# A graph and mixture-of-experts layer on one Trainium2 core: row distances moved from VectorE and ScalarE sweeps to TensorE turnings and products with ones

## The chip, the cores and the metric

The kernel runs on one core of a Trainium2 chip. The metric is device time in microseconds (us), the median of several executions. TensorE's matmuls are called PE in the rows, the weight loads before them PEld, VectorE DVE, ScalarE ACT, GpSimd POOL, and the queue of SyncE SP.

## The reference

The input is x, 12500 rows of 256 float32, and 200000 edges (src, dst), sorted by dst. The layer has two halves. What the change touches is in the first:

```python
mems  = layernorm(x)
mems2 = mems.at[y].set(r)                        # one row is overwritten by r
d2    = sum((mems2 - r)**2, axis=-1)             # distance of every row to r
nbr   = top_k(-d2, 7)                            # 7 nearest rows become edges into row y
deg   = segment_sum(keep, dst) + 2.0             # edges into y are dropped, the 7 added
dinv  = rsqrt(deg)
out   = segment_sum(dinv[src] * dinv[dst] * (mems2 @ W)[src], dst) + 2 * dinv**2 * (mems2 @ W)
x     = x + out
```

The second half is layernorm again, a gate that picks one of 8 experts per row, at most 1954 rows an expert, two matmuls 256 to 1024 to 256, and the result times its gate added to x.

## The kernel before, in words

The program is written by hand with semaphores: each engine has its own list of instructions, and each wait names a semaphore and a count. Nothing reorders it. The 12500 rows lie as 98 windows of 128 rows (`NW`) in one tile `nodes`, 128 partitions x 2 halves of 128 features (`KD`) x 98 windows x 128. Windows go in 7 chunks of 14 (`NZC`, `ZC`), or in 14 batches of 7 (`U`). `arena` is a tile that many buffers share in turn, and `columns` holds per-row numbers. The stages up to the first gather, which the change is about:

- SyncE loads edges and x (L495 to L518). TensorE turns the edges and their limits (L1701, L1708); VectorE copies them out (L984, L1001).
- VectorE works out bases and keys of the groups of edges from the limits (L1003 to L1063). In the middle it signals `bases`; TensorE spreads them over the partitions by three products with ones (L1711 to L1714, `cmp_ps`), and VectorE goes on with the keys.
- Then the row statistics (L1065 to L1097): `bn_stats` of 98 windows, ScalarE's root (L761), and scale and shift per row. Normalising in place: ScalarE windows 0 to 39 (`ACT_WIN`, L754), VectorE 40 to 97 (L1100). VectorE patches row y with r (L1105).
- Beside it GpSimd fetches 98 rows of sorted dst (L654), seven a batch, and ScalarE counts in them (`count_first`, L750), 9 batches (`EARLY`) ahead of the root and 5 between its normalising. When all 98 are counted (`less_ok`), VectorE and two products on TensorE (L1718, L1719) make the degrees, ScalarE their root, VectorE `dinv` (L1172, `deg_ok`).
- Distances and scaling, woven together: VectorE subtracts r from 7 windows (`differ`, L1114), ScalarE squares (L775), VectorE sums (`sum_squares`, L1122); and each chunk of `nodes` is multiplied by `dinv`, chunks 0, 2, 4, 6 on VectorE (L1181), 1, 3, 5 on ScalarE (L779). The scaled rows are called z. SyncE stores each chunk to `z_table` in DRAM as soon as it is scaled (L527).
- When a chunk is stored, TensorE turns its windows (L1743), and VectorE (L1195) and ScalarE (L790) write them back to `nodes` as the start of the sums.
- VectorE takes the 7 smallest distances in a few steps (L1203 to L1232) that run among the first gathers.

After that GpSimd gathers rows of `z_table` by src (L669), 4 tiles of 128 edges a step, 304 steps, with 4 buffers; TensorE adds each step up by a product with a selection matrix (L1776), VectorE adds it into `nodes` (L1248). GpSimd starts when all chunks are stored and all distances are done (L659 to L661). Convolution, layernorm, gate and routing run among the later steps, and the experts follow (L2017, L2029).

```python
            for c in range(NZC):
                pool.wait_ge(chunk_moved[c], STORED[c])
            pool.wait_ge(S["dist_ok"], 2 * NZC)
```

Of the kernel before, what the change touches and what calls it, by code (L numbers as in the profile page):

```python
# [10 lines left out]
P = 128  # L11


def build(nc, x, src, dst, gnn_r, gnn_w, yidx, gate_w, gate_b, w1, b1, w2, b2, out):
# [77 lines left out]
    ACT_WIN = 40  # L92
    EARLY = 9
    NEAR_PE, NEAR_DVE = (0, 4, 7), (2, 5, 8)
    DR = 4
    LAG = DR - 1

# [88 lines left out]
    with ctx:  # L186
# [10 lines left out]

        up_bank = [bank[2], bank[3], bank[6], bank[7]]
# [121 lines left out]
        at[0] = here - EB * P  # L320
        cross_row = carve([TILES])[0:1, :]
        at[0] = here + 16 * P // 2
# [10 lines left out]
        at[0] = 0  # L333
        diff = carve([DR, U, KD, P])

# [81 lines left out]
        dist = sb("dist", [P, NW])  # L417
        first_i = sb("first_i", [P, NW], I32)
# [39 lines left out]
        for name in ("""edges_cleared edges_in r_in y_in consts edges_float edge_psum edges_out lims limps lim_rows bases  # L458
                     cmp_ps hist_built hist_used hist_ps mean_sum square_ok ssum dst_rows_out last_built first_ok
                     first_in0 first_in1 half_ok starts_ok starts_ps hist_start less_ok bn1_ok shift_ok  # L460
                     piece_out piece_turned mem_ok mem_patched diff_ok dist_ok deg_ok z_ok z_act tick near_ok near_ps chosen_ok zT_ps
# [29 lines left out]
        def _(sp):  # L491
# [29 lines left out]
            for c in range(NZC):  # L521
                if c % 2:
                    sp.wait_ge(S["z_act"], (c + 1) // 2 * ZC)
                else:
                    sp.wait_ge(S["z_ok"], c // 2 + 1)
# [84 lines left out]
        def _(pool):  # L610
# [50 lines left out]
            pool.wait_ge(S["dist_ok"], 2 * NZC)  # L661
# [77 lines left out]
        def _(act):  # L739
            def node_row(w):  # L740
                return nodes[:, :, w, :]
# [11 lines left out]
            def normalise(w):  # L753
                nc.scalar.activation(node_row(w), node_row(w), ACT.Identity, bias=shift[:, w:w + 1],  # L754
                                     scale=rstd[:, w:w + 1]).then_inc(S["mean_sum"], 1)

            act.wait_ge(S["half_ok"], 1)
            for b in range(EARLY):
                count_first(b)
            act.wait_ge(S["ssum"], 1)  # L760
            nc.scalar.activation(dist[:, :], var2[:, :], ACT.Sqrt).then_inc(S["root_ok"], 1)  # L761
            act.wait_ge(S["shift_ok"], 1)
            part = -(-ACT_WIN // (2 * NZC - EARLY))
# [4 lines left out]
            act.wait_ge(S["mean_sum"], ACT_WIN)  # L768
            act.sem_inc(S["mem_ok"], 1)
            act.wait_ge(S["deg_ok"], 1)  # L770
            nc.scalar.activation(deg_root[:, :], deg[:, :], ACT.Sqrt).then_inc(S["root_ok"], 1)

            for b in range(2 * NZC):
                act.wait_ge(S["diff_ok"], KD * (b + 1))
                nc.scalar.activation(diff[:, b % DR, :, :, :], diff[:, b % DR, :, :, :], ACT.Square).then_inc(S["square_ok"], 1)  # L775
                if b % 4 == 3:
                    act.wait_ge(S["deg_ok"], 2)
                    for w in range(b // 2 * ZC, (b // 2 + 1) * ZC):
                        nc.scalar.activation(node_row(w), node_row(w), ACT.Identity, bias=zeros[:, 0:1],  # L779
                                             scale=dinv[:, w:w + 1]).then_inc(S["z_act"], 1)  # L780

            act.wait_ge(S["dst_kept"], 16)
            act.wait_ge(S["less_ok"], NW)
            nc.scalar.activation(counts_f, zeros[:, 0:1].to_broadcast([P, P * NW // 2]), ACT.Copy).then_inc(S["counts_clear"], 1)
# [9 lines left out]
            act.wait_ge(S["dist_ok"], 2 * NZC)  # L794
# [140 lines left out]
        def _(dve):  # L935
# [62 lines left out]
            for n in range(len(EDGE_TURNS)):  # L998
                i, b0, nb = EDGE_TURNS[n]
                dve.wait_ge(S["limps"], n + 1)  # L1000
                then(nc.vector.tensor_copy(lim_row[0:1, i, b0 * P:(b0 + nb) * P], bank[2 + n % 2][0:1, 0:nb * P]))  # L1001
                dve.sem_inc(S["lim_rows"], 1)
            lim_grp = lim_row[0:1, :, 0:TILES].rearrange("p i (g t) -> p i g t", t=GT)  # L1003
# [61 lines left out]
            dve.wait_ge(S["r_in"], 16)  # L1065
            then(nc.vector.memset(rel_b[:, TILES:EB * P], -1.0))
            then(nc.vector.tensor_single_scalar(wy_i[:, :], y_i[:, :], 7, ALU.arith_shift_right))
            then(nc.vector.tensor_scalar(is_y[:, :], node_id[:, :], y_f[:, 0:1], None, ALU.is_equal))
            then(nc.vector.tensor_scalar(not_y[:, :], is_y[:, :], -1.0, 1.0, ALU.mult, ALU.add))
            then(nc.vector.tensor_reduce(mine_y[:, :], is_y[:, :], AX.X, ALU.add))  # L1070
            then(nc.vector.tensor_scalar(r_y[:, :], r_rows[:, :], mine_y[:, 0:1], None, ALU.mult))
            then(nc.vector.tensor_scalar(invalid[:, :], node_id[:, :], float(N), -3.0e38, ALU.is_ge, ALU.mult))
            then(nc.vector.tensor_scalar(tok_id[:, :], node_id[:, :], 1.0, None, ALU.add))
            then(nc.vector.memset(taken_i[:, :], 0))


            for c in range(NZC):
                dve.wait_ge(chunk_moved[c], LOADED[c])
                for w in range(c * ZC, (c + 1) * ZC):
                    nc.vector.bn_stats(bn1[:, w, :], nodes[:, :, w, :]).then_inc(S["bn1_ok"], 1)  # L1080
            dve.wait_ge(S["bn1_ok"], NW)
            then(nc.vector.tensor_tensor(gap2[:, :], bn1[:, :, 1], bn1[:, :, 4], ALU.subtract))
            then(nc.vector.tensor_tensor(gap2[:, :], gap2[:, :], gap2[:, :], ALU.mult))
            then(nc.vector.tensor_tensor(var2[:, :], bn1[:, :, 2], bn1[:, :, 5], ALU.add))
            then(nc.vector.tensor_scalar(var2[:, :], var2[:, :], 1.0 / D, EPS, ALU.mult, ALU.add))
            then(nc.vector.scalar_tensor_tensor(var2[:, :], gap2[:, :], 0.25, var2[:, :], ALU.mult, ALU.add))
            dve.sem_inc(S["ssum"], 1)
            then(nc.vector.tensor_tensor(neg_mean[:, :], bn1[:, :, 1], bn1[:, :, 4], ALU.add))
            then(nc.vector.tensor_scalar(neg_mean[:, :], neg_mean[:, :], -0.5, None, ALU.mult))
            dve.wait_ge(S["root_ok"], 1)  # L1090
            then(nc.vector.reciprocal(rstd[:, :], dist[:, :]))
            then(nc.vector.tensor_tensor(gap2[:, :], rstd[:, :], rstd[:, :], ALU.mult))
            then(nc.vector.tensor_tensor(gap2[:, :], gap2[:, :], var2[:, :], ALU.mult))
            then(nc.vector.tensor_scalar(gap2[:, :], gap2[:, :], -0.5, 1.5, ALU.mult, ALU.add))
            then(nc.vector.tensor_tensor(gap2[:, :], gap2[:, :], not_y[:, :], ALU.mult))
            then(nc.vector.tensor_tensor(rstd[:, :], rstd[:, :], gap2[:, :], ALU.mult))
            nc.vector.tensor_tensor(shift[:, :], rstd[:, :], neg_mean[:, :], ALU.mult).then_inc(S["shift_ok"], 1)  # L1097
            dve.wait_ge(S["shift_ok"], 1)
            for w in range(ACT_WIN, NW):
                nc.vector.tensor_scalar(nodes[:, :, w, :], nodes[:, :, w, :], rstd[:, w:w + 1], shift[:, w:w + 1],  # L1100
                                        ALU.mult, ALU.add).then_inc(S["mem_ok"], 1)
            wy = dve.value_load(wy_i[0:1, 0:1], min_val=0, max_val=NW - 1)
            dve.wait_ge(S["mem_ok"], NW - ACT_WIN + 1)
# [4 lines left out]

            def differ(b):

                if b >= DR:
                    dve.wait_ge(S["dist_ok"], b - DR + 1)
                for k in range(KD):
                    nc.vector.tensor_tensor(diff[:, b % DR, :, k, :], nodes[:, k, b * U:(b + 1) * U, :],  # L1114
                                            r_rows[:, k * P:(k + 1) * P].unsqueeze(1).to_broadcast([P, U, P]),
                                            ALU.subtract).then_inc(S["diff_ok"], 1)
                if b >= LAG:
                    sum_squares(b - LAG)

            def sum_squares(b):  # L1120
                dve.wait_ge(S["square_ok"], b + 1)
                nc.vector.tensor_reduce(dist[:, b * U:(b + 1) * U], diff[:, b % DR, :, :, :], AX.XY, ALU.add).then_inc(S["dist_ok"], 1)  # L1122
# [20 lines left out]
            with dve.If(n_unsorted > 0):  # L1143
                nc.vector.tensor_copy(dst_i[:, :], dst_f[:, :]).then_inc(S["hist_start"], 1)
# [29 lines left out]
            differ(0)  # L1174
            differ(1)
            dve.wait_ge(S["deg_ok"], 2)
            for c in range(NZC):
                for k in range(KD if c % 2 == 0 else 0):
                    dve.wait_ge(S["diff_ok"], 2 * KD * (c + 1))
# [3 lines left out]
                if c % 2 == 0:  # L1183
                    ins.then_inc(S["z_ok"], 1)
# [900 lines left out]
```

## Time and profile before

| | |
|---|---|
| median of 3 runs | 2591.44 us (2588.29 to 2591.5) |
| the profiled execution | 2592.29 us |
| its span, first to last instruction | 2590.8 us |
| granted TensorE clock, mean | 0.888 |
| TensorE busy / weight loads | 1964.7 us (76%) / 1697.6 us (66%) |
| VectorE busy | 1318.2 us (51%) |
| ScalarE busy | 1011.5 us (39%) |
| GpSimd busy | 1548.2 us (60%) |
| first gather of z (L669) | at 246.96 us |

A page of a profile gives busy time as a mean over the whole span, and this program has stages with different limits. So the views used below are cut by time: the instructions of a stretch in order (the timeline, in which neighbours of one line are merged and "idle before" names what ended the wait), the groups of a line in a stretch, and the busy time of each engine in a stretch with the granted clock of TensorE. A clock of 1.00 is 2.4 GHz, 0.50 is 1.2 GHz.

### The profile page before, as it was taken

To read this page: it belongs to the slowest core of one execution; us is meant where nothing else is said; L and a number is where in the kernel's file an instruction comes from. 1 tells how busy PE (TensorE), PEld (TensorE's weight loads), DVE (VectorE), ACT (ScalarE), POOL (GpSimd) and SP (SyncE) were. 2 spreads that over 40 slices of the span, in tenths; PEclk is the share of its full clock that TensorE was granted. 3 is DMA by queue.
4 is the path that set the end of the run, shared out by engine and by line. 5 is a ranking of instruction groups with operands and counts; after the bars stand their busy time and mean duration, and the time that the engine had idled before them with its cause. 6 is when DMAs were issued, how large, how long until landed. Compare 5 with 4: busy or idle time off the path is not lost. (4 is left out here: it accounts for less than half of the span.)

```text
span 2590.8 us, 36610 instructions
## 1 busy us (share of the span) xinstructions
PE 1964.7 (76%) x11096; PEld 1697.6 (66%) x11096; DVE 1318.2 (51%) x3683; ACT 1011.5 (39%) x1769; POOL 1548.2 (60%) x1612
## 2 busy tenths in 40 slices
PE   2002777866786796786878888998599999999995
PEld 1002655855675585675767788887488788788875
DVE  7969875255325425335242257776444444454443
ACT  1377555345425525435343133333232323322332
POOL 6631777777777777777777777776223422422234
PEclk8555888988898898898989999999699999999998
DMA  9216433743473474573756777777512212212121
GB/s 264 66 57 181 120 103 115 259 136 104 152 253 106 128 254 128 165 240 104 238 166 206 229 213 208 210 208 173 143 33 71 83 36 71 76 36 71 42 68 28
DMA packets 235522, 359.05 MB, mean 139 GB/s; under 512 B 46585, under 2 KB 172697, under 8 KB 235221
## 3 DMA queue, kind: packets, MB, share of 16 engines
q0 software_dynamic: 74176, 194.10, 26.3%
q1 hardware_dynamic: 159860, 160.86, 20.2%
q10 hardware_dynamic: 1312, 2.10, 0.3%
q8 instruction: 71, 1.16, 0.2%
q14 instruction: 103, 0.84, 0.1%
HBM read 305.38 MB, written 56.40 MB: 140 GB/s over the span
## 5 line engine op out<-in xcount | busy, mean ns | idle before, releaser
L669 POOL DMA_INDIRECT arena<-z_table,arena x1216 | 1185.4, 975 | 462.0 <-issue 361.6
L1776 PE MATMUL bank<-arena 128*128 128x128 f32 x4864 | 711.0, 307 | 267.2 <-DMA arena<-z_table,arena 143.4
L1776 PEld LDWEIGHTS bank<-arena 128*128 128x128 f32 x4864 | 662.1, 218 | 364.3 <-issue 293.1
L1248 DVE TENSOR_TENSOR nodes<-nodes,bank 128x256 f32 x304 | 128.1, 421 | 755.8 <-PE bank L1776 740.8
L729 POOL DMA_INDIRECT out<-arena x128 | 130.7, 1021 | 419.1 <-DVE arena L1660 396.6
L2017 PE MATMUL bank<-arena 128*128 128x256 f32 (+1 forms) x1472 | 330.2, 384 | 14.2 <-DVE arena L1608 8.9
L927 ACT ACTIVATE nodes<-bank,arena 128x256 f32<-128x256 f32 (+1 forms) x368 | 152.7, 466 | 457.5 <-PE bank L2017 457.5
L2029 PE MATMUL bank<-arena,nodes 128*128 128x256 f32 (+1 forms) x1472 | 326.0, 379 | 0.0
L2017 PEld LDWEIGHTS bank<-arena 128*128 128x128 f32 x1472 | 282.7, 196 | 55.1 <-DVE arena L1608 10.9
L817 ACT ACTIVATE arena<-iota_h,arena 128x490 f16<-128x490 f16 x280 | 194.6, 695 | 304.3 <-PE bank L1788 304.3
L2029 PEld LDWEIGHTS bank<-arena,nodes 128*128 128x128 f32 (+1 forms) x1472 | 272.6, 187 | 40.1 <-issue 1.0
L1798 PE MATMUL bank<-arena,columns 128*128 128x256 f32 x1176 | 271.9, 381 | 2.7 <-ACT columns L807 2.7
L807 ACT ACTIVATE columns<-arena 128x768 f32<-128x768 uint16 (+3 forms) x102 | 153.1, 1506 | 262.2 <-PE bank L1798 258.8
L1798 PEld LDWEIGHTS bank<-arena,columns 128*128 128x128 f32 x1176 | 217.6, 192 | 29.2 <-issue 3.3
L1238 DVE TENSOR_TENSOR arena<-iota_b,arena 128x512 f32<-128x512 bf16 x304 | 208.5, 687 | 0.1
L819 ACT ACTIVATE arena<-arena,ones 128x490 bf16<-128x490 f16 x280 | 196.9, 703 | 9.1
L1268 DVE TENSOR_TENSOR arena<-arena,bank 128x490 f32 x280 | 184.8, 660 | 3.0 <-issue 1.3
L718 POOL DMA_INDIRECT arena<-x_rows,list_i x128 | 125.2, 978 | 98.9 <-DVEq L1597 49.8
L1608 DVE COPY arena<-bank 128x512 f32<-128x512 f32 (+1 forms) x46 | 31.2, 679 | 218.8 <-PE bank L1999 215.8
L1788 PE MATMUL bank<-arena 128*128 128x490 bf16 x352 | 119.4, 435 | 16.7 <-DVE arena L1268 14.9
L654 POOL DMA_INDIRECT arena<-dst_rows,first_i x98 | 100.7, 1027 | 52.1 <-issue 29.3
L1640 DVE TENSOR_TENSOR arena<-bank,arena 128x256 f32<-128x256 f32 x92 | 39.0, 424 | 146.9 <-PE bank L2029 142.7
(315 smaller groups left out, 1850.8 us busy)
## 6 DMA issues: line engine op xcount, KB each, us to landing
arena<-z_table SPq DMA_DIRECT2D x96, 768.0 KB, 4.6
arena<-z_table,arena POOLq DMA_INDIRECT x1216
arena<-in_L_ffn_w SPq DMA_DIRECT2D x14, 1024.0 KB, 7.0
z_table<-nodes SPq DMA_DIRECT2D x14, 896.0 KB, 6.7
x_rows<-nodes SPq DMA_DIRECT2D x98, 128.0 KB
arena<-in_x SPq DMA_DIRECT2D x48, 256.0 KB, 3.1
out<-nodes SPq DMA_DIRECT2D x96, 128.0 KB
nodes<-in_x SPq DMA_DIRECT2D x12, 896.0 KB, 11.5
```

The source lines that it names most:

```text
L669: nc.gpsimd.indirect_dma_start(gath[:, slot, t, :], None, z_table, bass.IndirectOffsetOnAxis(ap=src_idx[:, tile_at:tile_at + 1], axis=0)). ...
L729: nc.gpsimd.indirect_dma_start(out, bass.IndirectOffsetOnAxis(ap=out_idx[0:m, 2 * n + t:2 * n + t + 1], axis=0), o_tile[0:m, slot, :], Non ...
L807: nc.scalar.activation(count_f[:, j, 0:m, 0:nodes_in], counts[:, 0:nodes_in, c * HB:c * HB + m].rearrange("p n h -> p h n"), ACT.Copy).the ...
L817: nc.scalar.activation(far, iota_h[:, :], ACT.Abs, bias=neg_key[:, n:n + 1]).then_inc(S["key_ok"], 1)
L819: nc.scalar.activation(oh_key[:, n % 2, t, :], far, ACT.Relu, bias=ones[:, 0:1], scale=-1.0).then_inc(S["key_ok"], 1)
L927: nc.scalar.activation(hid[:, f, 0:n], up_bank[f // 2][:, f % 2 * CR:f % 2 * CR + n], ACT.Relu, bias=b1_pair[:, j * FT + f:j * FT + f + 1] ...
L1238: nc.vector.tensor_tensor(sel[:, step % SR, :, :], iota_b[:, :].unsqueeze(1).to_broadcast([P, GT, P]), rel_b[:, t0:t0 + GT].unsqueeze(2).t ...
L1268: nc.vector.tensor_tensor(where, where, strip_bank[n % 2][:, 0:PW], ALU.add).then_inc(S["strip_added"], 1)
L1776: last = nc.tensor.matmul(agg_bank[i][:, k * P:(k + 1) * P], gath[:, i, t, k * P:(k + 1) * P], sel[:, i, t, :], start=(t == 0), stop=(t == ...
L1798: last = nc.tensor.matmul(piece_bank[:, 0:D], count_f[:, j, i, :], z_ring[:, j, i, :], start=False, stop=False)
L2017: last = nc.tensor.matmul(up_bank[b][:, i * CR:i * CR + n], w1_sb[:, j, k, f * P:(f + 1) * P], xs_feat[:, s % 2, k, 0:n], start=(k == 0), ...
L2029: last = nc.tensor.matmul(bank[4 + t][0:m, 0:D], hid[:, f, t * P:t * P + m], w2_sb[:, j, f, :], start=(f == 0), stop=(f == FT - 1))
```

## The change

The distances are computed otherwise. VectorE no longer subtracts or sums. For each block of 4 windows (`NBK` = 25 blocks, the last of 2) TensorE turns the normalised windows, so that features lie on partitions (`turn_nodes`, two PSUM banks a block, two pairs in turn); ScalarE squares them out of PSUM with minus r as the bias per feature (`far_squares`, into 3 buffers `squares` in the arena); TensorE multiplies each squared 128 x 128 piece by a column of ones, which adds the features up into one column of `dist_bank` per window (`sum_squares`). Minus r per feature comes from turning r once. TensorE's order is turn block b, then sum block b - 1.

So that the rows are normalised early, the statistics are moved ahead of the keys, behind the limits' copies, and VectorE normalises all 98 windows. The bases' spread over partitions moves into TensorE's stream, behind turning block 20. ScalarE counts 6 batches before the root and 8 after it, with up to 4 blocks of squares behind each. Row y is patched only when all windows are turned. Chunks 2 and 5 of z are scaled by ScalarE, the other five by VectorE, one after the other. GpSimd no longer waits for the distances.

```diff
-    ACT_WIN = 40
-    EARLY = 9
+    EARLY = 6
+    NBK = -(-NW // 4)
+    SQ = 3
+    SPREAD_AT = 20
+    Z_ACT = (2, 5)
+    Z_DVE = [c for c in range(NZC) if c not in Z_ACT]
...
+        dist_bank = bank[7]
+        far_bank = [(bank[2], bank[3]), (bank[0], bank[6])]
...
 # gpsimd
-            pool.wait_ge(S["dist_ok"], 2 * NZC)
...
 # scalar
-            def normalise(w):
-                nc.scalar.activation(node_row(w), node_row(w), ACT.Identity, bias=shift[:, w:w + 1],
-                                     scale=rstd[:, w:w + 1]).then_inc(S["mean_sum"], 1)
+            def far_squares(b):
+                wide = P * min(4, NW - 4 * b)
+                act.wait_ge(S["nT_ps"], b + 1)
+                if b >= SQ:
+                    act.wait_ge(S["dist_ps"], b - SQ + 1)
+                for k in range(KD):
+                    nc.scalar.activation(squares[b % SQ][:, k, 0:wide], far_bank[b % 2][k][:, 0:wide], ACT.Square,
+                                         bias=neg_r[:, k:k + 1]).then_inc(S["square_ok"], 1)
...
             for b in range(EARLY, 2 * NZC):
-                for w in range((b - EARLY) * part, min((b - EARLY + 1) * part, ACT_WIN)):
-                    normalise(w)
                 count_first(b)
+                for n in range(4 * (b - EARLY), min(4 * (b - EARLY + 1), NBK)):
+                    far_squares(n)
...
-            for b in range(2 * NZC):
-                act.wait_ge(S["diff_ok"], KD * (b + 1))
-                nc.scalar.activation(diff[:, b % DR, :, :, :], diff[:, b % DR, :, :, :], ACT.Square).then_inc(S["square_ok"], 1)
-                if b % 4 == 3:
...
+            act.wait_ge(S["deg_ok"], 2)
+            for c in Z_ACT:
...
 # vector: the block from wait r_in to the statistics is moved from behind the keys to behind the limits, and ends with
-            for w in range(ACT_WIN, NW):
+            for w in range(NW):
                 nc.vector.tensor_scalar(nodes[:, :, w, :], nodes[:, :, w, :], rstd[:, w:w + 1], shift[:, w:w + 1],
                                         ALU.mult, ALU.add).then_inc(S["mem_ok"], 1)
...
-            dve.wait_ge(S["mem_ok"], NW - ACT_WIN + 1)
+            dve.wait_ge(S["mem_ok"], NW)
+            dve.wait_ge(S["nT_ps"], NBK)
...
-            differ(0)
-            differ(1)
             dve.wait_ge(S["deg_ok"], 2)
-            for c in range(NZC):
-                for k in range(KD if c % 2 == 0 else 0):
-                    dve.wait_ge(S["diff_ok"], 2 * KD * (c + 1))
+            for c in Z_DVE:
+                for k in range(KD):
                     rows = nodes[:, k, c * ZC:(c + 1) * ZC, :]
                     ins = nc.vector.tensor_tensor(rows, rows, dinv[:, c * ZC:(c + 1) * ZC].unsqueeze(2).to_broadcast([P, ZC, P]),
                                                   ALU.mult)
...
 # tensor
+            def turn_nodes(b):
+                pe.wait_ge(S["mem_ok"], min(4 * (b + 1), NW))
+                if b >= 2:
+                    pe.wait_ge(S["square_ok"], KD * (b - 1))
+                for k in range(KD):
+                    for i in range(min(4, NW - 4 * b)):
+                        last = nc.tensor.transpose(far_bank[b % 2][k][:, i * P:(i + 1) * P], nodes[:, k, 4 * b + i, :], ident[:, :])
+                last.then_inc(S["nT_ps"], 1)
+
+            def sum_squares(b):
+                pe.wait_ge(S["square_ok"], KD * (b + 1))
+                for i in range(min(4, NW - 4 * b)):
+                    w = 4 * b + i
+                    for k in range(KD):
+                        last = nc.tensor.matmul(dist_bank[:, w:w + 1], squares[b % SQ][:, k, i * P:(i + 1) * P], ones[:, 0:1],
+                                                start=(k == 0), stop=(k == KD - 1))
+                last.then_inc(S["dist_ps"], 1)
...
+            for b in range(NBK):
+                turn_nodes(b)
+                if b == SPREAD_AT:
+                    spread_bases()
+                if b:
+                    sum_squares(b - 1)
+            sum_squares(NBK - 1)
```

On TensorE, from the spread of the bases to the turning of z, the order before is (`row_start` are the counts, `nodes` at the end is z):

```order
L1712 MATMUL bank<-grp_cmp,ones 128x392 [waits bases]
L1713 MATMUL bank<-arena,ones 128x280
L1714 MATMUL bank<-ones,disorder 1x1
L1718 MATMUL bank<-row_start,down_one 128x98 [waits starts_ok]
L1719 MATMUL bank<-row_start,corner 128x98
```

With the change the same engine has this around the spread and at the end of the distances (`arena` with `ones` are the squares):

```order
L1716 MATMUL bank<-ident,nodes 128x128 [waits square_ok,mem_ok]
L1716 MATMUL bank<-ident,nodes 128x128 x7
L1700 MATMUL bank<-grp_cmp,ones 128x392 [waits bases]
L1701 MATMUL bank<-arena,ones 128x280
L1702 MATMUL bank<-ones,disorder 1x1
L1724 MATMUL bank<-ones,arena 128x1 [waits square_ok]
L1724 MATMUL bank<-ones,arena 128x1 x7
...
L1716 MATMUL bank<-ident,nodes 128x128 [waits square_ok,mem_ok]
L1716 MATMUL bank<-ident,nodes 128x128 x3
L1724 MATMUL bank<-ones,arena 128x1 [waits square_ok]
L1724 MATMUL bank<-ones,arena 128x1 x7
L1724 MATMUL bank<-ones,arena 128x1 [waits square_ok]
L1724 MATMUL bank<-ones,arena 128x1 x3
L1739 MATMUL bank<-row_start,down_one 128x98 [waits starts_ok]
```

Before, the two products of the degrees came right behind the spread; now 196 turnings and 196 products with ones stand ahead of them in TensorE's queue, and the spread stands among these.

On VectorE, at the patch of row y and behind `dinv`, the order before is:

```order
L1105 ISA [waits mem_ok]
L1105 TENSOR_TENSOR nodes<-nodes,r_y 128x128
...
L1172 TENSOR_TENSOR dinv<-dinv,columns 128x98 [waits dve_ch]
L1114 TENSOR_TENSOR arena<-nodes,r_rows 128x7x128 x4
L1181 TENSOR_TENSOR nodes<-nodes,dinv 128x1792 [waits diff_ok,deg_ok]
L1181 TENSOR_TENSOR nodes<-nodes,dinv 128x1792 [waits diff_ok]
L1114 TENSOR_TENSOR arena<-nodes,r_rows 128x7x128 x4
L1122 TENSOR_REDUCE dist<-arena 128x7 [waits square_ok]
```

and with the change:

```order
L1115 ISA [waits nT_ps,mem_ok]
L1115 TENSOR_TENSOR nodes<-nodes,r_y 128x128
...
L1168 TENSOR_TENSOR dinv<-dinv,columns 128x98 [waits dve_ch]
L1174 TENSOR_TENSOR nodes<-nodes,dinv 128x1792 [waits deg_ok]
L1174 TENSOR_TENSOR nodes<-nodes,dinv 128x1792 x9
L1181 TENSOR_SCALAR nodes<-bank 128x2x128 [waits zT_ps,chunk_moved0] x7
```

The patch now waits for the turnings as well, and behind `dinv` VectorE has the scaling of five chunks alone, with the writing back of the turned windows right behind it.

## Rows read from the trace of the kernel before

**Rows 1.** The groups of one line, L669: instructions, shortest/median/longest ns, first and last start.

```profile
L669 POOL DMA_INDIRECT arena<-z_table,arena x1216: 942/946/2245, 247.0 to 1806.7; - x174
```

**Rows 2.** GpSimd's timeline, 240:274: start, duration, line, [idle <- its end].

```profile
272.01 0.94 POOL L669 DMA_INDIRECT arena<-z_table,arena  x1 [5.34 <-PE bank L1776]
```

**Rows 3.** Timeline of all engines, 160 to 248 us.

```profile
164.66 0.18 ACT L750 ACTIVATION_READ_ACCUMULATOR arena<-arena,columns 128x1 f32 x1
...
165.69 0.74 PE L1718 MATMUL bank<-row_start,down_one 128*128 128x98 f32 x2 [88.40 <-DVEq L1128]
...
170.86 0.26 DVE L1172 TENSOR_TENSOR dinv<-dinv,columns 128x98 f32<-128x98 f32 x1
...
175.23 3.96 DVE L1181 TENSOR_TENSOR nodes<-nodes,dinv 128x1792 f32<-128x1792 f32 x2
...
179.22 60.87 SPq L527 DMA_DIRECT2D z_table<-nodes  x14
...
233.11 3.96 DVE L1181 TENSOR_TENSOR nodes<-nodes,dinv 128x1792 f32<-128x1792 f32 x2
...
246.96 0.94 POOL L669 DMA_INDIRECT arena<-z_table,arena  x1 [86.78 <-DMA z_table<-nodes]
```

**Rows 4.** Groups by line, 20:270: xcount | busy, mean ns | idle before.

```profile
L1114 DVE TENSOR_TENSOR arena<-nodes,r_rows 128x896 f32<-128x896 f32 x28 | 29.1, 1087 | 0.3
L1122 DVE TENSOR_REDUCE dist<-arena 128x7 f32<-128x1792 f32 x14 | 28.0, 2014 | 0.0
```

**Rows 5.** Timeline of VectorE, 10 to 270 us.

```profile
50.79 1.10 DVE L1001 COPY arena<-bank 1x512 f32<-1x512 f32 x2 [0.20 <-PE bank L1708]
...
73.90 0.56 DVE L1043 SCALAR_TENSOR_TENSOR grp_cmp<-grp_bad,grp_base 1x392 f32<-1x392 f32 x1
77.33 0.30 DVE L1046 TENSOR_TENSOR arena<-arena,bank 128x144 f32<-128x144 f32 x1 [2.87 <-PE bank L1714]
...
86.00 0.14 DVE L1066 MEMSET arena<- 128x96 bf16 x1
...
88.51 32.11 DVE L1080 BATCH_NORM_STATS2 arena<-nodes 128x6 f32<-128x256 f32 x98
...
125.95 19.69 DVE L1100 TENSOR_SCALAR nodes<-nodes,columns 128x256 f32<-128x256 f32 x58
```

**Rows 6.** Stretches: busy us of PE, PEld, DVE, ACT, POOL; clock, DMA.

```profile
195.00:200.00 5.00, 0.00 (x0) 0.00 (x0) 5.00 (x5) 0.85 (x1) 0.00 (x0) 0.50 1.00 286
```

**Rows 7.** Timeline of weight loads, 1834 to 1843 us.

```profile
1834.75 0.87 PEld L1872 LDWEIGHTS bank<-ident,arena 128*128 128x128 f32 x4
1835.60 1.83 PEld L1881 LDWEIGHTS bank<-arena 128*128 128x128 f32 x8
...
1840.33 1.83 PEld L1881 LDWEIGHTS bank<-arena 128*128 128x128 f32 x8
1842.03 0.97 PEld L1900 LDWEIGHTS bank<-arena 128*128 128x128 f32 x4
```

**Rows 8.** Timeline of weight loads, 1603 to 1608 us.

```profile
1605.25 0.97 PEld L1881 LDWEIGHTS bank<-arena 128*128 128x128 f32 x8
1606.14 1.87 PEld L1776 LDWEIGHTS bank<-arena 128*128 128x128 f32 x16
```

**Rows 9.** Stretches, the turning of z (L1743) alone: busy PE, busy PEld, clock, DMA.

```profile
244.00:247.00 3.00, 3.00 (x16) 3.00 (x15) 0.50 0.55 159
...
251.00:255.00 4.00, 4.00 (x40) 4.00 (x38) 1.00 0.41 109
```

**Rows 10.** Stretches, all engines, columns as in rows 6.

```profile
340.00:390.00 50.00, 36.10 (x199) 27.00 (x200) 31.15 (x93) 24.54 (x37) 38.12 (x40) 0.84 0.36 103
1600.00:1610.00 10.00, 8.84 (x70) 8.20 (x68) 9.19 (x25) 1.64 (x4) 8.17 (x7) 1.00 0.76 207
1831.00:1843.00 12.00, 8.93 (x40) 8.50 (x40) 7.51 (x36) 4.56 (x7) 0.00 (x0) 0.51 0.12 10
```

**Rows 11.** One line, L851, an eviction of 128x512 from PSUM by ScalarE.

```profile
L851 ACT ACTIVATE arena<-bank x49: 571/598/601, 1495.9 to 1836.1; 128x512 f32<-128x512 f32 x49
```

More of the change, by code:

```diff
@@ L319, in build @@
         stage_f2 = carve([EB, P])
-        at[0] = here - EB * P
+        at[0] = 0
         cross_row = carve([TILES])[0:1, :]
+        squares = []
+        for begins in (here - EB * P, here, here + 16 * P // 2 + U * P):
+            at[0] = begins
+            squares.append(carve([KD, 4 * P]))
+        assert at[0] <= here + (2 * 16 * (P + NW)) // 2
         at[0] = here + 16 * P // 2
@@ new lines, in _ @@
+            then(nc.vector.tensor_scalar(r_y[:, :], r_rows[:, :], mine_y[:, 0:1], None, ALU.mult))
+            then(nc.vector.tensor_scalar(invalid[:, :], node_id[:, :], float(N), -3.0e38, ALU.is_ge, ALU.mult))
+            then(nc.vector.tensor_scalar(tok_id[:, :], node_id[:, :], 1.0, None, ALU.add))
+            then(nc.vector.memset(taken_i[:, :], 0))
+            for c in range(NZC):
+                dve.wait_ge(chunk_moved[c], LOADED[c])
+                for w in range(c * ZC, (c + 1) * ZC):
+                    nc.vector.bn_stats(bn1[:, w, :], nodes[:, :, w, :]).then_inc(S["bn1_ok"], 1)
@@ new lines, in _ @@
+            dve.wait_ge(S["bn1_ok"], NW)
+            then(nc.vector.tensor_tensor(gap2[:, :], bn1[:, :, 1], bn1[:, :, 4], ALU.subtract))
+            then(nc.vector.tensor_tensor(gap2[:, :], gap2[:, :], gap2[:, :], ALU.mult))
+            then(nc.vector.tensor_tensor(var2[:, :], bn1[:, :, 2], bn1[:, :, 5], ALU.add))
+            then(nc.vector.tensor_scalar(var2[:, :], var2[:, :], 1.0 / D, EPS, ALU.mult, ALU.add))
+            then(nc.vector.scalar_tensor_tensor(var2[:, :], gap2[:, :], 0.25, var2[:, :], ALU.mult, ALU.add))
@@ new lines, in _ @@
+            dve.sem_inc(S["ssum"], 1)
+            then(nc.vector.tensor_tensor(neg_mean[:, :], bn1[:, :, 1], bn1[:, :, 4], ALU.add))
+            then(nc.vector.tensor_scalar(neg_mean[:, :], neg_mean[:, :], -0.5, None, ALU.mult))
+            dve.wait_ge(S["root_ok"], 1)
+            then(nc.vector.reciprocal(rstd[:, :], dist[:, :]))
+            then(nc.vector.tensor_tensor(gap2[:, :], rstd[:, :], rstd[:, :], ALU.mult))
+            then(nc.vector.tensor_tensor(gap2[:, :], gap2[:, :], var2[:, :], ALU.mult))
@@ new lines, in _ @@
+            then(nc.vector.tensor_scalar(gap2[:, :], gap2[:, :], -0.5, 1.5, ALU.mult, ALU.add))
+            then(nc.vector.tensor_tensor(gap2[:, :], gap2[:, :], not_y[:, :], ALU.mult))
+            then(nc.vector.tensor_tensor(rstd[:, :], rstd[:, :], gap2[:, :], ALU.mult))
+            nc.vector.tensor_tensor(shift[:, :], rstd[:, :], neg_mean[:, :], ALU.mult).then_inc(S["shift_ok"], 1)
+            dve.wait_ge(S["shift_ok"], 1)
+            for w in range(NW):
+                nc.vector.tensor_scalar(nodes[:, :, w, :], nodes[:, :, w, :], rstd[:, w:w + 1], shift[:, w:w + 1],
+                                        ALU.mult, ALU.add).then_inc(S["mem_ok"], 1)
@@ L1081, in _ @@
[L1081 to L1086, printed above, removed]
@@ L1182, in _ @@
                                                   ALU.mult)
-                if c % 2 == 0:
-                    ins.then_inc(S["z_ok"], 1)
-                if c + 1 < NZC:
-                    differ(2 * (c + 1))
-                    differ(2 * (c + 1) + 1)
-            for b in range(2 * NZC - LAG, 2 * NZC):
-                sum_squares(b)
+                ins.then_inc(S["z_ok"], 1)
             for w in range(0, NW, 2):
@@ L1200, in _ @@
             ycol = dve.value_load(y_i[0:1, 0:1], min_val=0, max_val=N - 1)
-            dve.wait_ge(S["dist_ok"], 2 * NZC)
-            then(nc.vector.scalar_tensor_tensor(near[:, :], dist[:, :], -1.0, not_y[:, :], ALU.mult, ALU.mult))
+            dve.wait_ge(S["dist_ps"], NBK)
+            then(nc.vector.scalar_tensor_tensor(near[:, :], dist_bank[:, 0:NW], -1.0, not_y[:, :], ALU.mult, ALU.mult))
             then(nc.vector.tensor_tensor(near[:, :], near[:, :], invalid[:, :], ALU.add))
@@ L1710, in _, with spread_bases @@
                 last.then_inc(S["limps"], 1)
-            pe.wait_ge(S["bases"], 1)
-            nc.tensor.matmul(bank[4][:, 0:GROUPS], ones[0:1, :], grp_cmp[0:1, :], start=True, stop=True)
-            nc.tensor.matmul(bank[5][:, 0:UN], ones[0:1, :], unit_cmp, start=True, stop=True)
-            nc.tensor.matmul(bank[4][0:1, GROUPS:GROUPS + 1], disorder[:, :], ones[:, 0:1], start=True, stop=True).then_inc(S["cmp_ps"], 1)
+            def spread_bases():
+                pe.wait_ge(S["bases"], 1)
+                nc.tensor.matmul(bank[4][:, 0:GROUPS], ones[0:1, :], grp_cmp[0:1, :], start=True, stop=True)
+                nc.tensor.matmul(bank[5][:, 0:UN], ones[0:1, :], unit_cmp, start=True, stop=True)
+                nc.tensor.matmul(bank[4][0:1, GROUPS:GROUPS + 1], disorder[:, :], ones[:, 0:1],
+                                 start=True, stop=True).then_inc(S["cmp_ps"], 1)
@@ new lines, in _ @@
+            pe.wait_ge(S["r_in"], 16)
+            for k in range(KD):
+                last = nc.tensor.transpose(bank[5][:, k * P:(k + 1) * P], r_rows[:, k * P:(k + 1) * P], ident[:, :])
+            last.then_inc(S["r_ps"], 1)
+            def turn_nodes(b):
[6 more added lines that the diff above has]
+                last.then_inc(S["nT_ps"], 1)
```

88 lines of the change are left out of this document (27 added, 61 removed).

## The prediction, made before the changed kernel ran

> **What bounds the kernel now.** I read the gathers first, because every later stage consumes them. GpSimd issues 1216 of them, from 247.0 to 1806.7 us [rows 1], one each 1.25 us with next to no other wait; what follows the last one lasts as long as before, whenever it starts. So the time is the moment of the first gather, plus a chain that this change does not touch, plus the waits inside the chain. There is one such wait worth naming: after 16 gathers GpSimd stands for 5.3 us until TensorE has added up the first group [rows 2], since TensorE could not begin before VectorE and ScalarE had refilled `nodes`. The first gather waits for the last store of the scaled rows z, 86.8 us long [rows 3].
>
> Next, what sets that store. VectorE runs without a gap from the limits (L1001) over the keys to the row statistics and the normalised rows [rows 5]. Then it stands until ScalarE's last count of edges (L750) ends at 164.8 us; the small chain from there to `dinv` ends at 171.1 us [rows 3]. From 171 to 243 us VectorE alternates scaling and distances: 28 subtractions and 14 sums, 57 us [rows 4]. So the stores, which start at 179.2 us, are issued over 61 us [rows 3], though they move 286 GB/s where z is there in time [rows 6]. TensorE has nearly nothing to do in this stage.
>
> **What leaves the path.** The 57 us of subtractions and sums go, and ScalarE's squares of them. VectorE now scales five chunks of 14 windows in a row, about 4.0 us each [rows 3], and ScalarE two beside it. The stores then are bound by the DMA: 14 of 896 KB, 12.85 MB at 286 GB/s [rows 6], 45 us, against 20 us of scaling. The first is issued 4.0 us after `dinv`, not 8. So from `dinv` to the first gather it takes 4.0 + 45 + 1.5 = 50.5 us in place of 75.9. The 1.5 us for the landing is a choice: today the last scaling ends at 237.1 us, its two stores need 6.4, and the gather starts at 247.0 [rows 3]; the 3.5 us left over are partly a queue, so the landing lies between 0 and 3.5. Refilling `nodes` now follows the stores chunk by chunk, and TensorE's first group comes some 7 us after the first gather (the last chunk's refill of 14 windows, keys and a transfer), not 21: the wait of 5.3 us shrinks to the usual 0.3, and 5.0 are won.
>
> **What comes onto the path.** The distances go to TensorE, and `dinv` has to wait for them twice: VectorE's patch of row y stands behind the last turning of all windows (`nT_ps`), and in TensorE's own queue the two products that give the degrees (L1718) stand behind the last sum. The count:
>
> Start: the moved block (2.5 us, 86.0 to 88.5), the statistics (32.1) and the small chain behind (5.3) follow the limits at 51.9 us, and the first four normalised windows take 4 x 0.34 us [rows 5]: 93.2 us. The loads of `nodes` are no wait.
>
> Passes: 196 turnings leave one pass each. The 196 products with a column of ones have float32 operands, and this trace shows such a product as two passes, each with its own load of 128 columns of weights: 392. In all 588 passes, with weights that are used once. Their pace depends on the clock. At the half level (granted 0.50, 1.2 GHz) four turnings take 0.85 us, and eight passes of the thin products of the gate (128x8, the nearest to 128x1) take 1.70: 0.213 us each for both kinds [rows 7]. At the full level (1.00, 2.4 GHz) eight thin passes take 0.89 us, 0.111 each [rows 8, 10], and turnings 0.100 [rows 9]. The stream takes 588 x 0.213 = 125.2 us at half, 392 x 0.111 + 196 x 0.100 = 63.1 us at full. These are the bounds; no row shows this mixture in a long run.
>
> Which level? The clock rises when TensorE does nothing but turn z without a gap: 0.50 in 244 to 247, 1.00 in 251 to 255 [rows 9]. It holds its full level for most of the gather stage too, 0.84 on average from 340 to 390 with TensorE busy for 36.1 of 50 us, mostly with passes of 128 columns and more [rows 10]. But from 1831 to 1843, busy for as large a share and without a pause in the last 4 us, it stood at the half level [rows 10]: there 16 of the 40 passes are thin ones of 8 columns [rows 7, 10]. In the new stream two thirds of the passes move one column, 16 after every 8 turnings. I take the half level for the whole stream. The Trainium skill ("TensorE: Matmul & The Clock Gate", Why this matters for your kernels) says that a TensorE kept busy without pauses gets its full clock; rows 10 speak against it for thin passes, though no row shows them for long; by that rule the stream would take 63 us and not 125. The same page (Part 4: PE-mode transpose) says that turnings do not lift the clock at all; rows 9 show the opposite, so a lift at the start stays possible.
>
> The keys: TensorE spreads the bases (2.9 us with its waits [rows 5]) after turning block 20, at about 194 us; VectorE has them ready at 125.1 + 22.6 = 147.7 (98 windows of normalising end at 91.8 + 33.3; from the limits to the bases it is 51.9 to 74.5 today). It stands from there to some 197 and then needs at most the 11.5 us that today lie between the bases and 86.0 [rows 5], done by 209, before the last turning ends at 216. Hidden; if the stream were faster, this would be the next thing to wait for.
>
> ScalarE: per block two squares of 128x512 out of PSUM, as the eviction of that size, 0.60 us [rows 11], and 2.8 us of counting per four blocks: 7.6 us against 20.5 of TensorE. Hidden. Its last count waits behind the squares of block 24 and ends at about 220 us, just ahead of TensorE. GpSimd's gathers for the counts (L654) are held back by this, but stay ahead of it: seven of them take 8.75 us at the pace of 1.25.
>
> Sum: 93.2 + 125.2 + 2.9 = 221.3 us for the end of the stream. Then 5.4 us from the first degree product to `dinv` [rows 3]: 226.7 us in place of 171.1. Plus 50.5: the first gather at 277.2 us against 246.96, 30.2 later; less 5.0 for the wait: 25.2 us more. The profiled execution took 2592.29 us (span 2590.8), so 2617.5; the median of the runs is 0.85 lower, so I predict **2616 us**, 1.0% slower.
>
> The bounds of this case: at the start two blocks of turnings (16 passes) follow each other before the first thin pass. If they lift the clock for a few us, some 60 passes run at full: 6 us less. A wait of up to 0.3 us at each of the 25 handovers between TensorE and ScalarE adds up to 7.5, and if the wait of 5.0 is not won it comes back. 2608 to 2629.
>
> **The rivals.** Full clock: if the mixture keeps the clock up once lifted, the stream no longer decides. After the spread of the bases at 148 us 116 passes are left, so it would end at about 162, and ScalarE's last count would end as today, at 165. `dinv` stays at 171.1, the first gather comes at 171.1 + 50.5 = 221.6, 25.4 earlier, and 5.0 are won: 30.4 less, 2561 us. For it: the engine is never idle, and turnings alone do lift the clock. Against it: the stretch of thin passes [rows 10]. It decides from 0.17 us a pass on, where the stream is 25 us shorter and the loss is gone.
>
> The clock alternates: in the gather stage it stands at 0.84 on average [rows 10]. With half of the passes at each level the stream takes 94 us, 31 less than in the forecast: 2586 us, about 0.2% under today. Against it: there the passes that lift it again are wide, and here their share never changes.
>
> The work doesn't move as said: if the patch and L1718 did not stand behind the stream, TensorE's 125 us would lie beside the stores, until the 7 nearest are chosen, and the gain of the first rival would be had at either clock. The order above speaks against it: both waits are in the program. No chance of its own.
>
> **How the numbers follow.** Half level 0.78, full 0.12, alternating 0.10. About 0.2%, 5 us, is what a measurement can tell from no change. The alternating case is spread over both sides: 0.04 of it faster, 0.04 the same, 0.02 slower. Faster 0.16, same 0.04, slower 0.80. The range has to take in the half level whole and reaches down to the middle of the alternating case: 2590 to 2630; the likeliest case alone has 2608 to 2629.
>
> **What would show it.** In the profile after: TensorE's granted clock 0.50 in 110 to 215 us, with TensorE busy without a gap; turnings and thin products at 0.21 us a pass; the thin products the largest new group; VectorE idle until `cmp_ps` and then until `nT_ps`; stores over some 45 us at over 280 GB/s; the first gather near 277 us and no wait of 5 us behind it. Wrong: a granted clock near 1.00 in that stretch and the first gather before 230 us; passes under 0.2 us at the half clock; a last count that ends long after the stream.

## The result and the profile after

| | before | after |
|---|---|---|
| median, the runs right behind the prediction | 2591.47 us (4 runs) | 2616.33 us (4 runs, 2610.89 to 2618.17) |
| median, a second comparison | 2591.89 us (9 runs) | 2614.36 us (5 runs, 2610.85 to 2620.93) |
| after : before, 95% interval | | 1.009 [1.0074, 1.0106]; again 1.0086 [1.0071, 1.010] |
| the profiled execution, its span | 2592.29 us, 2590.8 us | 2610.89 us, 2609.4 us |
| first gather of z, last gather | 246.96 us, 1806.7 us | 272.56 us, 1827.4 us |

The change makes the kernel 0.9% slower. In the changed kernel L1716 is a turning of a window, L767 a square, L1724 a product with ones, L1739 the first product of the degrees, L1168 `dinv`, L535 the stores of z, L676 the gathers, L788 ScalarE's scaling, L757 a count of edges, L1092 the first step of VectorE behind the spread of the bases.

First the gathers. The answer to [rows 1], with GpSimd's waits for TensorE in all 1216 of them (us, times), the same waits in the kernel before, and the seventeenth gather as in [rows 2]:

```profile
L676 POOL DMA_INDIRECT arena<-z_table,arena x1216: 942/946/2242, 272.6 to 1827.4; - x174
...
  PE bank L1797: 10.4, 34
```

```profile
  PE bank L1776: 13.6, 28
```

```profile
293.66 1.01 POOL L676 DMA_INDIRECT arena<-z_table,arena  x1 [0.30 <-issue]
```

They start 25.6 us later and end 20.7 later, so 4.9 us are won between the first and the last. The stall of 5.34 us behind the sixteenth gather [rows 2] is gone: the next one follows after 0.30. But GpSimd's waits for TensorE fall by 3.2 us only, from 13.6 to 10.4, since others have come in; the rest of the 4.9 is spread over the gathers. From the last gather to the end it takes 782.0 us, 2.1 less than before, and no cause of that is shown. So 25.6 - 4.9 - 2.1 = 18.6 us, the difference of the two spans.

Next, why the first gather is late. Stretches of the changed kernel, columns as in [rows 6]:

```profile
100.00:110.00 10.00, 10.00 (x50) 10.00 (x49) 10.00 (x31) 5.22 (x18) 5.85 (x6) 0.50 0.13 39
150.00:160.00 10.00, 10.00 (x49) 10.00 (x49) 0.00 (x0) 2.53 (x4) 4.72 (x5) 0.50 0.13 39
200.00:210.00 10.00, 10.00 (x50) 10.00 (x49) 0.00 (x0) 4.65 (x16) 0.00 (x0) 0.50 0.00 0
230.00:240.00 10.00, 0.00 (x0) 0.00 (x0) 10.00 (x6) 10.00 (x11) 0.00 (x0) 0.59 1.01 284
```

TensorE is busy for 10 of 10 us from 100 to 210 us, at a granted clock of 0.50 (three of eleven such rows stand here). ScalarE works there for a quarter to a half of the time, and VectorE stands from 145 to 191 us. Behind it, from 230 us, TensorE has nothing to do and the DMA moves 284 GB/s at a share of 1.01: the stage of the stores. The groups from 90 to 216 us say what TensorE did:

```profile
L1724 PEld LDWEIGHTS bank<-ones,arena 128*128 128x128 f32 x392 | 84.5, 326 | 0.2 <-ACT arena L767 0.2
...
L1716 PEld LDWEIGHTS bank<-ident,nodes 128*128 128x128 f32 x196 | 41.9, 241 | 42.1 <-issue 42.1
```

The products' weight loads are 84.5 us of the stretch, twice the 41.9 of the turnings'; a pass takes 0.216 us of one and 0.214 of the other (84.5 / 392 and 41.9 / 196). TensorE waited 0.2 us for the squares in the whole stream. The timeline around its end, and on to the first gather:

```profile
191.28 0.30 DVE L1092 TENSOR_TENSOR arena<-arena,bank 128x144 f32<-128x144 f32 x1 [46.23 <-PE bank L1702]
...
204.42 1.76 PEld L1716 LDWEIGHTS bank<-ident,nodes 128*128 128x128 f32 x8
...
209.44 0.90 PEld L1716 LDWEIGHTS bank<-ident,nodes 128*128 128x128 f32 x4
...
210.32 5.24 PEld L1724 LDWEIGHTS bank<-ones,arena 128*128 128x128 f32 x24
...
215.45 0.55 PEld L1739 LDWEIGHTS bank<-row_start,down_one 128*128 128x128 f32 x2
...
220.67 0.26 DVE L1168 TENSOR_TENSOR dinv<-dinv,columns 128x98 f32<-128x98 f32 x1
...
224.95 40.87 SPq L535 DMA_DIRECT2D z_table<-nodes  x14
...
272.56 0.94 POOL L676 DMA_INDIRECT arena<-z_table,arena  x1 [76.30 <-DMA z_table<-nodes]
```

A block goes from 204.42 to 209.44: 24 passes in 5.02 us, 0.209 each. VectorE's 46.23 us of idle time ahead of 191.28 are the wait for the spread of the bases. The last sums start behind the last turnings at 210.3, the degrees' product at 215.45, with no gap between. `dinv` is ready at 220.93, 5.5 us later; the first store is issued 4.0 us behind that, the fourteen of them over 40.9 us, and the first gather follows at 272.56.

### The profile page after: what moved, and what is told of

Its sections match the earlier page's. It is cut to its first block and busy times, and to the rows that moved or that the text cites. A ratio compares the mean times of both kernels' runs of the same rounds, so it can differ in the third digit from the quotient of the medians.

```text
span 2609.4 us, 37803 instructions
## 1 busy us (share of the span) xinstructions
PE 2087.5 (80%) x11686; PEld 1816.3 (70%) x11686; DVE 1275.6 (49%) x3683; ACT 992.2 (38%) x1752; POOL 1547.0 (59%) x1612
## 5 line engine op out<-in xcount | busy, mean ns | idle before, releaser
L676 POOL DMA_INDIRECT arena<-z_table,arena x1216 | 1185.7, 975 | 446.4 <-issue 359.8
L2050 PEld LDWEIGHTS bank<-arena,nodes 128*128 128x128 f32 (+1 forms) x1472 | 272.6, 187 | 40.1 <-issue 1.0
```

Of the source, the lines that this page charges most:

```text
L676: nc.gpsimd.indirect_dma_start(gath[:, slot, t, :], None, z_table, bass.IndirectOffsetOnAxis(ap=src_idx[:, tile_at:tile_at + 1], axis=0)). ...
L2050: last = nc.tensor.matmul(bank[4 + t][0:m, 0:D], hid[:, f, t * P:t * P + m], w2_sb[:, j, f, :], start=(f == 0), stop=(f == FT - 1))
```

## The experiments

Theory A is the prediction's: the thin products hold TensorE at its half clock, its 588 passes at that clock are the path to `dinv`, and behind `dinv` the DMA bounds. Theory B: the pace comes from loading new weights for each pass, and the level of the clock in this stretch has nothing to do with what the products move.

**The changed kernel once more.** No edit. Its first profile was the shortest of the four runs, so it was asked where the other 5 us are.

> The changed kernel unchanged, for a second profile. Its first profiled execution took 2610.89 us and is the shortest of four; the other three lie between 2616.27 and 2618.17. In that profile TensorE had its full clock for some us at the start of the distances (granted 0.67 from 90 to 100 us, 0.50 from 100 to 215). Theory: whether the first turnings lift the clock there differs from run to run and is worth about 5 us; then a profile of about 2616 us shows 0.50 from 92 us on and a first gather at about 278 us instead of 272.6. Rival: the difference lies behind the gathers, and the first gather is at 272.6 us again. Median expected: 2616, 2611 to 2619.

Measured: 2620.93 us in the profile, median 2614.36. Three stretches of the first profile, and the same three of this one:

```profile
92.00:95.00 3.00, 2.62 (x13) 2.65 (x14) 3.00 (x10) 0.64 (x2) 2.28 (x3) 0.50 0.16 44
95.00:98.00 3.00, 3.00 (x26) 2.80 (x25) 3.00 (x11) 1.90 (x4) 2.39 (x3) 0.96 0.22 66
98.00:102.00 4.00, 4.00 (x25) 4.00 (x23) 4.00 (x14) 1.26 (x2) 3.08 (x4) 0.58 0.16 49
```

```profile
92.00:95.00 3.00, 1.30 (x6) 1.33 (x7) 2.96 (x10) 0.00 (x0) 2.27 (x3) 0.50 0.14 44
95.00:98.00 3.00, 3.00 (x16) 2.95 (x15) 3.00 (x11) 1.89 (x4) 2.39 (x3) 0.50 0.21 66
98.00:102.00 4.00, 4.00 (x21) 4.00 (x21) 4.00 (x14) 0.64 (x2) 3.08 (x4) 0.50 0.15 49
```

In the first profile the sixteen turnings with which the stream begins had lifted the clock (0.96 from 95 to 98), and it was back at the half level within 3 us of the first product. In the second the stream began 1.3 us later and the clock was never lifted. The gathers of the second:

```profile
L676 POOL DMA_INDIRECT arena<-z_table,arena x1216: 942/946/2241, 276.6 to 1835.1; - x174
```

The first comes 4.0 us later than in the first profile, 1.3 by the later start and 2.7 by the lift that did not come, as the theory has it (it said 278); but the last comes 7.7 later, since the gathers themselves took 1558.5 us and not 1554.8, and 2.3 more lie behind them. So about 4 of the 10 us between the two profiles are the clock's and the start's; the rest is spread over the gathers and the stages behind, and no cause of it is shown.

**128 columns of ones instead of one.**

```diff
-    nc.tensor.matmul(dist_bank[:, w:w + 1], squares[b % SQ][:, k, i * P:(i + 1) * P], ones[:, 0:1],
+    nc.tensor.matmul(dist_bank[:, w:w + 128], squares[b % SQ][:, k, i * P:(i + 1) * P], ones[:, 0:128],
```

The sum then stands in 128 columns; the 127 to the right are overwritten by the windows that follow, so nothing else in the kernel changes.

> The same 392 products in the same order with the same weights, but each moves 128 columns of ones instead of one (the 127 further columns land to the right of the window's column and are overwritten by the next window). Theory A, the thin passes hold TensorE at the half clock, and the stream at that clock is what dinv waits for: the granted clock goes to 1.00 by about 105 us, a pass takes 0.10 to 0.12 us, the stream ends near 160 us, dinv comes at about 171 us and the first gather at 171 + 51.6 = 223 us; the time falls by the 50 us that dinv comes earlier, to 2566 us (2558 to 2574). Theory B, the pace is that of loading new weights for each pass, and the clock in this stretch doesn't depend on what is moved: 0.21 us a pass again, no gain, 2616 us, or some us more.

Measured: 2562.84 us, 0.9892 of the kernel before, [0.9877, 0.9907], and so 2.0% under the change as it was. Two of its stretches, the weight loads of one block, and the timeline from the last count on:

```profile
100.00:110.00 10.00, 10.00 (x91) 9.90 (x91) 10.00 (x32) 6.85 (x22) 7.21 (x7) 1.00 0.16 48
150.00:160.00 10.00, 10.00 (x93) 10.00 (x92) 7.82 (x12) 5.38 (x15) 7.02 (x7) 1.00 0.15 47
```

```profile
100.61 0.91 PEld L1716 LDWEIGHTS bank<-ident,nodes 128*128 128x128 f32 x8
101.49 1.86 PEld L1724 LDWEIGHTS bank<-ones,arena 128*128 128x128 f32 x16
103.27 0.91 PEld L1716 LDWEIGHTS bank<-ident,nodes 128*128 128x128 f32 x8
```

```profile
164.30 0.20 ACT L757 ACTIVATION_READ_ACCUMULATOR arena<-arena,columns 128x1 f32 x1
...
165.36 0.50 PEld L1739 LDWEIGHTS bank<-row_start,down_one 128*128 128x128 f32 x2 [2.52 <-DVEq L1123]
...
170.53 0.26 DVE L1168 TENSOR_TENSOR dinv<-dinv,columns 128x98 f32<-128x98 f32 x1
...
174.81 40.85 SPq L535 DMA_DIRECT2D z_table<-nodes  x14
...
222.43 0.95 POOL L676 DMA_INDIRECT arena<-z_table,arena  x1 [63.58 <-DMA z_table<-nodes]
```

The clock is 1.00 from 100 us to the end of the stream and 91 passes fit into 10 us where 50 did. A block of 24 passes takes 2.66 us, 0.111 a pass, with 128 times as many columns moved by the products. `dinv` is ready at 170.8, 50.1 us earlier than with one column, and the first gather comes 50.1 earlier, at 222.43. So Theory B is out in what it says of the clock: the weights, their number and their order are the same, and the clock went up with what the products move, and the pace with it. That a pass takes as long as the loading of its weights is not refuted: at the full clock it took 0.111 us with 8 columns [rows 8] and with 128. What `dinv` waits for now is ScalarE's last count: it ends at 164.5, and the degrees' product follows at 165.36, 2.3 us after TensorE's last sum. That is where it stood in the kernel before (164.66 in [rows 3]).

**32 columns.** The same edit with 32 for 128.

> The same with 32 columns of ones, a quarter of what a turning moves. Theory A leaves open where between one and 128 columns the clock turns: either the full clock as with 128 columns (2566 us), the half clock as with one (2616 us), or the full clock for a part of the stream (in between, with a granted clock that changes once or several times between 100 and 215 us). Theory B: 2616 us.

Measured: 2567.98 us, 0.9913 of before [0.9892, 0.9934]. Its stretches, and the weight loads where the clock changes:

```profile
140.00:150.00 10.00, 10.00 (x85) 9.14 (x85) 6.26 (x18) 6.36 (x20) 6.56 (x7) 1.00 0.14 44
150.00:160.00 10.00, 10.00 (x52) 10.00 (x51) 6.60 (x8) 2.53 (x4) 6.48 (x6) 0.52 0.14 43
```

```profile
143.71 1.86 PEld L1724 LDWEIGHTS bank<-ones,arena 128*128 128x128 f32 x16
145.41 0.94 PEld L1716 LDWEIGHTS bank<-ident,nodes 128*128 128x128 f32 x8
146.52 0.29 PEld L1700 LDWEIGHTS bank<-grp_cmp,ones 1*128 1x128 f32 x2 [0.17 <-issue]
...
147.84 0.09 PEld L1702 LDWEIGHTS bank<-ones,disorder 128*1 128x1 f32 x2 [0.37 <-issue]
...
150.72 3.54 PEld L1724 LDWEIGHTS bank<-ones,arena 128*128 128x128 f32 x16
154.00 1.76 PEld L1716 LDWEIGHTS bank<-ident,nodes 128*128 128x128 f32 x8
```

The full clock up to 150 us, the half clock from there: sixteen product passes take 1.70 us at 143.71 and 3.28 at 150.72. Between lies the spread of the bases (146.52 to 147.96), three products whose weights come from one partition or one column. Behind it the stream of turnings and 32-column products did not bring the clock back, though TensorE was busy for 10 of 10 us. It costs 4.7 us against 128 columns: `dinv` is ready at 175.5.

**The spread behind the last turnings.** That kernel with `SPREAD_AT = 24` for 20.

> With 32 columns of ones, as before, but the spread of the bases stands behind turning block 24, the last, instead of block 20. With the spread at block 20 the granted clock was 1.00 from 100 to 149 us and 0.50 from 151 us on, that is from the spread on. Theory: the spread (three products from one partition, with waits between them) is what let the clock fall, and products of 32 columns hold a clock that they have but don't lift it; then the clock is 1.00 until about 158 us now, and the turnings and sums end near 160 us instead of 170. Rival: the clock falls in the same place or at another one without the spread. The time says little: the keys (9 us on VectorE) now follow the spread at the end, so dinv is expected at about 175 us as with the spread at block 20, and 2568 us.

Measured: 2563.07 us, one run, 5 us under what was expected, a difference on which one run says little. Its stretches, and the timeline at the end of the keys:

```profile
100.00:120.00 20.00, 20.00 (x182) 19.61 (x181) 20.00 (x62) 14.12 (x43) 13.72 (x14) 1.00 0.16 48
...
150.00:160.00 10.00, 10.00 (x85) 9.14 (x84) 1.74 (x5) 7.08 (x26) 4.95 (x6) 1.00 0.13 40
160.00:170.00 10.00, 2.63 (x12) 2.33 (x11) 7.27 (x13) 1.86 (x10) 0.00 (x0) 0.50 0.00 0
```

```profile
158.12 0.30 DVE L1092 TENSOR_TENSOR arena<-arena,bank 128x144 f32<-128x144 f32 x1 [13.43 <-PE bank L1702]
...
166.34 0.14 DVE L1109 CAST unsorted_i<-cross_sum 1x1 int32<-1x1 f32 x1
...
168.91 0.50 PEld L1739 LDWEIGHTS bank<-row_start,down_one 128*128 128x128 f32 x2 [7.51 <-DVEq L1123]
...
174.08 0.26 DVE L1168 TENSOR_TENSOR dinv<-dinv,columns 128x98 f32<-128x98 f32 x1
```

The clock stays at 1.00 until 160 us and falls behind the spread again; the distances end at 161.4. So in these two profiles, one of each kernel, the fall moved with the spread, and it was not the time that had passed. With 128 columns the same spread, at block 20, left the clock at 1.00 (the stretch from 150 us above). `dinv` is late for the expected reason: VectorE gets the spread at 158.1 and ends the keys at 166.5, and only then patches row y and makes the degrees.

**Each product twice.**

```diff
-                    for k in range(KD):
+                    for k in list(range(KD)) * 2:
```

> Each product of the squares with one column of ones is issued twice (the second time starts the sum anew, so the result is the same): 392 passes more on the half clock, at 0.209 us each (5.01 us a block of 24 passes in the profile of the changed kernel). If the stream is the path, each of them costs what it takes: 82 us more, 2698 us, dinv at about 303 us. Rival: ScalarE's last count or the bases, not the stream, sets dinv, and part of the 82 us lies beside them: under 60 us more.

Measured: 2699.65 us, one run. The groups of the products' weight loads and of the gathers (shortest, median and longest ns, first and last start):

```profile
L1724 PEld LDWEIGHTS bank<-ones,arena x784: 186/333/337, 96.0 to 299.2; 128*128 128x128 f32 x196
```

```profile
L676 POOL DMA_INDIRECT arena<-z_table,arena x1216: 942/946/2237, 356.7 to 1915.6; - x174
```

784 product passes instead of 392. The first gather moves from 272.6 to 356.7 us, by 84.1, and the time by 83.3 from the median of 2616.33; 82 were expected, and under 60 by the rival, which is out. So a pass of this stream costs the kernel its full 0.21 us, and nothing of it lies beside other work.

**Chunks 1, 3 and 5 of z on ScalarE, with 128 columns.** `Z_ACT = (1, 3, 5)` for `(2, 5)`, the assignment of the kernel before.

> With 128 columns of ones; chunks 1, 3 and 5 of z are scaled by ScalarE as in the kernel before, instead of 2 and 5. Theory: behind dinv the DMA bounds the stage (14 stores in 40.9 us at 284 GB/s), and who scales which chunk is hidden behind them: chunk 1 is then ready some 8 us after dinv, as chunk 0's stores end, so the first gather stays at dinv + 51 to 53 us and the time at 2563 us (2559 to 2567). Rival: the assignment of chunks is a part of the gain; then a store waits for a chunk, and up to 25 us come back.

Measured: 2565.33 us, 0.9893 of before [0.9875, 0.9912]: the same as with (2, 5), 0.9892 (the kernel before beside these last two kernels: 2594.63 us). The timeline behind `dinv`, and a stretch among the stores:

```profile
171.58 20.75 ACT L788 ACTIVATE nodes<-nodes,zeros,dinv 128x256 f32<-128x256 f32 x42 [1.97 <-DVE dinv L1168]
175.56 41.52 SPq L535 DMA_DIRECT2D z_table<-nodes  x14
...
223.28 0.95 POOL L676 DMA_INDIRECT arena<-z_table,arena  x1 [63.68 <-DMA z_table<-nodes]
```

```profile
185.00:190.00 5.00, 0.69 (x2) 0.29 (x2) 3.47 (x6) 5.00 (x11) 0.00 (x0) 0.50 1.00 280
```

ScalarE scales for 20.75 us instead of 13.87, and the stores take 41.5 us from the first issue to the last instead of 40.9, at 280 GB/s and more. From `dinv` (171.54) to the first gather it is 51.7 us. Who scales is hidden behind the stores.

## Why the prediction was right

**The likeliest case came as described.** Its steps against the first profile:

- *Start of the stream, 93.2 us:* 92.35.
- *588 passes at 0.213 us, at the half clock throughout:* 0.209 at the half clock, and for some 3 us at the start the full one, the lift that the bounds of the case had named as 6 us less. Here it was worth 2.7 (the stream took 123.1 us, and 125.8 in the second profile, where the lift did not happen).
- *End of the stream, 221.3 us:* 215.45. Of the 5.9 us, 0.8 are the start, 2.3 the pace (125.8 us in the second profile for the 128.1 of the sum), 2.7 the lift. In the second profile, without the lift and 1.3 us later at the start, it ended at 219.5.
- *From the first degree product to `dinv`, 5.4 us:* 5.5.
- *From `dinv` to the first gather, 50.5 us:* 51.6. The first store at 4.0, as said; the landing was set too short, at 1.5 us in a range of 0 to 3.5. With 45 us for the moving it was 2.6.
- *The stall of 5.0 us is won:* the stall is gone, but what the stage of the gathers gains by it is less sure: 4.9 us between first and last gather in the first profile, 5.5 with 128 columns, 1.2 in the second profile and 0.8 with each product twice. GpSimd's waits for TensorE are lower by 3 to 5 us in all of them; what makes up the rest is not shown.
- *The keys are hidden:* VectorE got the spread at 191.3 us (said 194) and ended with the keys at 199.9, ahead of the last turnings.
- *ScalarE's last count ends just ahead of TensorE:* about 1 us ahead. With 128 columns, where nothing else held it, the degrees' product followed 0.9 us behind that count; so here the stream was the later of the two by an estimated 0.3 us.

The sum for the profiled execution was 2617.5 us; it took 2610.89. Of the 6.6 us less, 5.9 are the earlier end of the stream and 2.1 the stretch behind the last gather, which the prediction had left as it was; 1.2 between `dinv` and the first gather go the other way. The median, 2616.33, meets the forecast of 2616 closer than the steps do, and that is luck: single runs lie between 2610.85 and 2620.93.

**The rival of the full clock was right in its price.** It was put at 2561 us, with the end of the stream at 162, `dinv` at 171.1 and the first gather at 221.6. With 128 columns these were 2562.84, 163.0, 170.8 and 222.43. From `dinv` to the first gather it took 51.6 us at either clock, in place of 75.8. So the gains that the change has on VectorE's and the DMA's side are there in either case, some 29 us with those of the gathers; whether the kernel is slower or faster is decided by the level of TensorE's clock in one stretch of 120 us.

**The half level came, but the argument for it was weaker than it looks.** It was taken from a stretch of the old kernel, 1831 to 1843 us, in which thin products stood among other passes [rows 10]. That stretch follows a pause of TensorE, and just before the pause sixteen passes of 8 columns had run at the full clock:

```profile
1826.00:1831.00 5.00, 3.39 (x26) 3.07 (x24) 3.45 (x16) 0.81 (x2) 0.00 (x0) 1.00 0.69 193
```

```profile
1827.42 1.97 PE L1881 MATMUL bank<-arena 128*128 128x8 f32 x16
1832.40 1.09 PE L1872 MATMUL bank<-ident,arena 128*128 128x128 f32 x4 [3.00 <-issue]
```

So those rows could not tell thin products from pauses, and that the level came as chosen is in part luck. The experiments do tell them apart: in the new stream, without pauses, a lifted clock came down within 3 us, and the same stream with 128 columns kept it up. The Trainium skill ("TensorE: Matmul & The Clock Gate", Why this matters for your kernels) has a TensorE that is kept busy at its full clock; the stretches from 100 to 210 us, busy for 10 of 10 us at 0.50, disagree, and those with 128 columns, at 1.00, agree. The Trainium skill also says, on the same page (Part 4: PE-mode transpose), that turnings don't lift the clock. That was in doubt by [rows 9], and the first profile contradicts it again: 0.96 right behind sixteen turnings.

**The case of an alternating clock** did not come with one column. With 32 it came in another form: full up to the spread of the bases, half behind it.

Not tried: taking the degrees and the patch of row y out from behind the stream at the half clock (the patch writes a window that is known only when the program runs, and the turnings read all of them).

## What to carry to other kernels

Work that is moved to an idle TensorE is not free because the engine is idle: count its passes, price them at both levels of the clock, and look who waits for the last one. Before a product with a very narrow moving operand is given up as slow, widen it into columns that later products overwrite: here 127 more columns a pass cost no time and gave back the clock, and 0.9% slower became 1.1% faster than the kernel before. And look at what stands in the middle of such a stream: with 32 columns, three small products were enough to lose the full clock for the rest of it; with 128 columns they were not.

## What was not expected of the hardware

- The same stream can run at either level, by what went before. With 32 columns the same blocks ran at 0.109 us a pass (2.61 us for 24) up to the spread and at 0.209 behind it.
- A stretch in which the profile shows TensorE busy for all of the time can stand at the half clock for 110 us.
- Whether the clock was lifted at the start of the stream changed from one execution of the same kernel to the next.
